# Expert layers: the output bias as a product of TensorE in place of sums of VectorE

## The chip, the cores and the metric

The kernel runs on one core of one Trainium2 chip. The metric is the device time of one execution in microseconds, the median of several runs.

## The reference

A small network of four blocks works on x of shape 16 x 96 x 16 x 16 (4096 tokens of 96 channels). Each block is a convolution or an attention part and then a feed-forward part, each added to its input. In the first three blocks the feed-forward part is a layer of four experts, which this change concerns:

```python
scores = jnp.einsum('bsd,de->bse', x, gate_w) + gate_b
probs = jax.nn.softmax(scores, axis=-1)
topk_vals, topk_idx = jax.lax.top_k(probs, TOP_K)
mask = jnp.sum(jax.nn.one_hot(topk_idx, NUM_EXPERTS, dtype=probs.dtype), axis=-2)
masked = probs * mask
masked = masked / (jnp.sum(masked, axis=-1, keepdims=True) + 1e-09)
h = jax.nn.gelu(jnp.einsum('bsd,edh->ebsh', x, w1) + b1[:, None, None, :], approximate=False)
y = jnp.einsum('ebsh,ehd->ebsd', h, w2) + b2[:, None, None, :]
out = jnp.einsum('bse,ebsd->bsd', masked, y)
```

The layer's x is the layer-normed token, DIM is 96, HID is 384, there are 4 experts and the best 2 count; the kernel computes all four and lets the gate be zero. The output bias `b2` is a row of 96 numbers for each expert, and every token receives it times its gate.

## The kernel before

The tokens X stay in SBUF as 32 tiles of 128 tokens x 96 channels. The function `moe` does one expert layer in 8 steps of 4 tiles (512 tokens). Each engine has its own program; they meet at semaphores. The first step and the last are written out, the six between them are a loop of two steps an iteration.

TensorE in step g, for experts e = 1, 2, 3: the up products of expert e (`ups`: 3 blocks of 128 hidden units, each as three reduced-precision products of 512 columns, L933 to L935), then the down products of expert e-1 (`downs`: 12 fp32 products of 96 columns, L943, into one of two PSUM banks `dn`). After the down products of expert 1 comes `turn` (L915), the transposes of the next step's normed tokens `xn`, and after the up products of expert 3 come the next step's gate products (L922). The up products of the next step's expert 0 and the down products of expert 3 end the step. The next stage's own first work stands in the last step (`follow`).

ScalarE makes the gelu (L878) between up and down products, and copies the turned tokens to `xt` and `xh`.

VectorE in step g: the 16 bias sums (`bias_sums`, L819: X = b2 * gate + X, a tile and expert each), the statistics of the next step's tokens (`stats_of`, L72 to L81), expert 0's sum (`expert_sum`, L827: X = down product * gate + X, four tiles), the normed tokens (`apply_of`, L88 to L91, which waits for a power on GpSimd, L773), expert 1's sum, the low part of the turned tokens (L806), the gates of the next step (L412 to L444, with an exponential on GpSimd, L777), and the sums of experts 2 and 3. The semaphore `added` counts the expert sums; TensorE's down products of expert e wait for the sum of expert e-2, which frees their bank.

In layer 0 the first step's statistics, tokens and gates are made inside the layer, before its steps. In layers 1 and 2 they are made in the stage before. So TensorE begins layer 1 and 2 at once with the up products of expert 0.

Of the kernel before, what the change touches and what calls it, by code (L numbers as in the profile page):

```python
# [12 lines left out]
F32 = mybir.dt.float32  # L13
# [5 lines left out]
P = 128  # L19
# [22 lines left out]
def wait(eng, sem, count):  # L42

    if isinstance(count, int) and count <= 0:
        return
    eng.wait_ge(sem, count)
# [662 lines left out]
def moe(nc, T, A, layer, follow=None):  # L709

    w1, w2, gw, b2 = T["moe"][layer]
    X, ident, F = T["X"], T["ident"], T["front"]
    w1h, w1l, xn, xt, xh, xl, gate = F.w1h, F.w1l, F.xn, F.xt, F.xh, F.xl, F.gate
# [2 lines left out]
    with ExitStack() as ctx:  # L718
        s = Scope(nc, ctx, f"moe{layer}")
        hid = s.sb("hid", [P, NE * KC, GW])  # L720
        up = [s.psum(f"up{i}", [P, 512]) for i in range(UPS)]
        tp = s.psum("tp", [P, 512])
        gp = s.psum("gp", [P, 512])
        dn = [s.psum(f"dn{i}", [P, 512]) for i in range(2)]
        scores = gp[:, 0:GT * NE]
        names = ("consts", "var_done", "rstd_done", "logit_done", "exp_done", "dve_step", "xn_done", "turned",
                 "xt_done", "xl_done", "gates_in", "gates_read", "up_done", "hid_done", "down_done", "added")
        (consts, var_done, rstd_done, logit_done, exp_done, dve_step, xn_done, turned, xt_done, xl_done, gates_in,
         gates_read, up_done, hid_done, down_done, added) = (s.sem(n) for n in names)
        if layer == 0:  # L730
            F.begin(s, T, 0, tp, scores)
        if follow:
# [54 lines left out]
        @block.vector  # L787
        def _(dve):

            STATS, APPLY, GATES = 4, 2, 15  # L790
            EACH = STATS + APPLY + GATES + 2 * NE

            def stats_of(g, chain):
                layernorm_stats(dve, chain, [X[:, GT * g + j, :] for j in range(GT)], F.stats, F.mean, F.var, 1e-5)
                dve.sem_inc(var_done, 1)  # L795

            def apply_of(g, chain):
                wait(dve, rstd_done, g)
                wait(dve, turned, g - 1)
                layernorm_apply(dve, chain, [X[:, GT * g + j, :] for j in range(GT)],  # L800
                                [xn[:, j, :] for j in range(GT)], F.stats, F.mean, F.rstd).then_inc(xn_done, 1)

            def low_of(g, p):

                wait(dve, xt_done, g)
                dve.tensor_tensor(xl[0:C, p, :], xt[0:C, p, :], xh[0:C, p, :].bitcast(F32), ALU.subtract  # L806
                                  ).then_inc(xl_done, 1)

            def gates_of(g, p, chain):
                wait(dve, gates_in, g)  # L810
                gate_logits(dve, chain, F, scores.rearrange("p (t e) -> p t e", e=NE), logit_done, gates_read)
                choose_experts(dve, chain, F, p, exp_done, g)

            def bias_sums(g, p, chain):

                for e in range(NE):
                    for j in range(GT):
                        x = X[:, GT * g + j, :]
                        last = dve.scalar_tensor_tensor(out=x, in0=b2[:, e, :], scalar=gate[:, p, j, e:e + 1], in1=x,  # L819
                                                        op0=ALU.mult, op1=ALU.add)  # L820
                    chain.sync(last)

            def expert_sum(g, p, e, chain):
                wait(dve, down_done, NE * g + e + 1)
                for j in range(GT):
                    x = X[:, GT * g + j, :]
                    last = dve.scalar_tensor_tensor(out=x, in0=dn[e % 2][:, j * C:(j + 1) * C],  # L827
                                                    scalar=gate[:, p, j, e:e + 1], in1=x, op0=ALU.mult, op1=ALU.add)
                chain.sync(last)
                dve.sem_inc(added, 1)  # L830

            def step(g, p, last):
                chain = Chain(dve, dve_step, base + g * EACH)
                begun = follow if last else None
                ahead = Chain(dve, follow.step) if begun else None
                if begun:
                    begun.dve_sums(dve, ahead)
                bias_sums(g, p, chain)
                if not last:
                    stats_of(g + 1, chain)  # L840
                if begun:
                    begun.dve_tokens(dve, ahead)
                expert_sum(g, p, 0, chain)
                if not last:
                    apply_of(g + 1, chain)
                expert_sum(g, p, 1, chain)
                if not last:
                    low_of(g + 1, 1 - p)
                    gates_of(g + 1, 1 - p, chain)
                if begun:  # L850
                    begun.dve_weights(dve, ahead)
                expert_sum(g, p, 2, chain)
                expert_sum(g, p, 3, chain)
                assert chain.n == (2 * NE if last else EACH), chain.n

            chain = Chain(dve, dve_step)
            if layer == 0:
                F.dve_stats(dve, chain)
                F.dve_apply(dve, chain)
                for e in range(NE):  # L860
                    F.dve_weights(dve, e)
                    if e == 0:
                        F.dve_low(dve)
                F.dve_logits(dve, chain)
                F.dve_gates(dve, chain)
            dve.wait_ge(T["moe_in"][layer], 64)
            base = chain.n
            steps(dve, step)

# [40 lines left out]
        def _(pe):  # L910
# [15 lines left out]
            def ups(g, p, e):  # L926
                if e == 0:
                    wait(pe, xl_done, g)
                for k in range(KC):
                    n = e * KC + k  # L930
                    wait(pe, hid_done, NE * KC * g + n - UPS + 1)
                    bank = up[n % UPS][:, :]
                    pe.matmul(bank, w1h[:, n, :], xh[:, p, :], start=True, stop=False)  # L933
                    pe.matmul(bank, w1l[:, n, :], xh[:, p, :], start=False, stop=False)  # L934
                    pe.matmul(bank, w1h[:, n, :], xl[:, p, :], start=False, stop=True).then_inc(up_done, 1)  # L935

            def downs(g, e):
                wait(pe, hid_done, NE * KC * g + (e + 1) * KC)
                wait(pe, added, NE * g + e - 1)
                for j in range(GT):  # L940
                    for k in range(KC):
                        n = e * KC + k
                        last = pe.matmul(dn[e % 2][:, j * C:(j + 1) * C], hid[:, n, j * P:(j + 1) * P], w2[:, n, :],  # L943
                                         start=(k == 0), stop=(k == KC - 1))
                last.then_inc(down_done, 1)

            def step(g, p, last):
# [20 lines left out]
            if layer == 0:  # L968
# [2 lines left out]
                pe.wait_ge(F.w_low, 1)  # L971
                pe.wait_ge(F.xl_done, 1)
            ups(0, 0, 0)
            steps(pe, step)
            if follow:
                stay_awake(pe, up[0], ident, 11)
# [1718 lines left out]
```

## Time and profile before

| | |
|---|---|
| time, median of 3 runs | 1303.06 us (1302.83 to 1305.04) |
| profiled execution | 1306.18 us, its span 1304.0 us |
| mean granted clock of TensorE | 0.952 |
| TensorE matmul busy | 1180.7 us, 91% |
| VectorE busy | 808.3 us, 62% |
| ScalarE busy | 482.9 us, 37% |
| GpSimd busy | 252.6 us, 19% |
| bias sums L819, VectorE | 384 instructions, 102.6 us |

The times come from one profiled execution. Matmul records overlap one another, so two that follow directly start closer than their duration. PEld is TensorE's weight load. "Idle before" is the time in which the engine stood still ahead of an instruction, and the arrow names what ended it. An fp32 product shows as two records.

### The profile page before, as it was taken

What the parts mean: (1) busy time and instruction counts of PE and PEld (TensorE: products, weight loads), DVE (VectorE), ACT (ScalarE), POOL (GpSimd) and SP (SyncE); (2) the same over time, 40 slices, a digit from 0 to 9 for tenths busy, and PEclk for the clock granted to TensorE, in tenths of its full rate; (3) what the DMA queues carried; (4) which work ended last, traced back from release to release, by engine and by line L of the source; (5) the groups of instructions that cost most, each with busy time, mean ns of one, the idle gap of its engine ahead of it and who ended that gap; (6) DMA issues with size and microseconds to landing.
All of it is one profiled execution on the core that took longest, in us unless ns stands there. A gap on an engine that the chain in (4) does not pass through costs nothing. (4 is left out here: it accounts for less than half of the span.)

```text
span 1304.0 us, 24105 instructions
## 1 busy us (share of the span) xinstructions
PE 1180.7 (91%) x8520; PEld 1029.8 (79%) x8520; DVE 808.3 (62%) x2930; ACT 482.9 (37%) x944; POOL 252.6 (19%) x234
## 2 busy tenths in 40 slices
PE   2979999957999999999999999999999997999776
PEld 1978888946999999888897767768988886888555
DVE  6036676736566664676666576654767667676656
ACT  3514333413455544333331323233333332232552
POOL 3002212122010100312121443332121212211200
PEclk9998999976999999899998999999999999999786
DMA  3201000010000000000000000000000000000000
GB/s 133 84 5 65 18 25 23 1 49 1 2 2 1 2 1 2 1 1 0 0 1 1 2 1 2 2 1 2 2 0 0 0 1 1 1 2 1 4 10 37
DMA packets 11562, 15.69 MB, mean 12 GB/s; under 512 B 7385, under 2 KB 9007, under 8 KB 11346
## 3 DMA queue, kind: packets, MB, share of 16 engines
q1 hardware_dynamic: 10754, 12.86, 3.0%
q10 hardware_dynamic: 720, 1.66, 0.3%
q8 instruction: 55, 0.90, 0.3%
q14 instruction: 33, 0.27, 0.1%
HBM read 11.37 MB, written 3.15 MB: 11 GB/s over the span
## 5 line engine op out<-in xcount | busy, mean ns | idle before, releaser
L943 PEld LDWEIGHTS moe_dn<-all_w,moe_hid 128*128 128x128 f32 x2304 | 269.9, 192 | 5.4
L943 PE MATMUL moe_dn<-all_w,moe_hid 128*128 128x96 f32 x2304 | 271.7, 275 | 0.0
L878 ACT ACTIVATE moe_hid<-moe_up 128x512 f32<-128x512 f32 x288 | 169.9, 599 | 231.6 <-PE moe_up L935 219.2
L933 PE MATMUL moe_up<-front_xh,front_w1h 97*128 97x512 f32 x288 | 122.4, 425 | 0.7 <-PEq L1474 0.4
L935 PE MATMUL moe_up<-front_xl,front_w1h 97*128 97x512 f32 x288 | 114.0, 396 | 0.0
L827 DVE SCALAR_TENSOR_TENSOR all_X<-moe_dn,front_gate,all_X 128x96 f32 (+1 forms) x384 | 95.2, 310 | 29.3 <-PE moe_dn L943 24.6
L934 PE MATMUL moe_up<-front_xh,front_w1l 97*128 97x512 f32 x288 | 113.4, 394 | 0.0
L819 DVE SCALAR_TENSOR_TENSOR all_X<-all_b,front_gate,all_X 128x96 f32 (+1 forms) x384 | 102.6, 329 | 13.9 <-DVE all_X L827 7.6
L1371 PE MATMUL l1c_o<-l1c_vs,l1c_pt 128*128 128x64 f32 x768 | 94.4, 277 | 0.5 <-DVE l1c_ro L1149 0.5
L1371 PEld LDWEIGHTS l1c_o<-l1c_vs,l1c_pt 128*128 128x128 f32 x768 | 91.8, 195 | 2.9 <-issue 0.9
L1115 DVE TENSOR_REDUCE l1c_nmax<-l1c_sc 128x2 f32<-128x512 f32 x96 | 61.8, 685 | 40.8 <-PE l1c_sc L1338 40.1
L777 POOL TENSOR_TENSOR front_prob<-front_euler,front_logit 128x16 f32<-128x16 f32 x21 | 60.9, 2902 | 122.3 <-DVEq L414 122.3
L1613 DVE SCALAR_TENSOR_TENSOR l2c_val<-third_xp,all_l_taps,l2c_val 96x544 f32<-96x544 f32 x64 | 64.5, 1008 | 13.8 <-ACT l2c_val L1689 11.2
L2056 DVE SCALAR_TENSOR_TENSOR l3c_ykv<-fourth_xp,all_l_taps,l3c_ykv 96x256 f32<-96x256 f32 x128 | 65.3, 510 | 4.0
L1781 PE MATMUL l2c_qp<-third_xp,third_diag 96*96 96x512 f32 x144 | 66.6, 598 | 0.0
L2182 PE MATMUL l3c_qp<-fourth_xp,fourth_wqt 96*128 96x256 f32 x288 | 66.1, 383 | 0.0
L1259 ACT ACTIVATE l1c_pt<-l1c_st 128x512 f32<-128x512 f32 x96 | 52.2, 595 | 36.9 <-PE l1c_st L1355 35.8
L935 PEld LDWEIGHTS moe_up<-front_xl,front_w1h 97*128 97x128 f32 x288 | 54.7, 190 | 12.6
L773 POOL TENSOR_TENSOR front_rstd<-front_var,front_mhalf 128x4 f32<-128x4 f32 x21 | 21.2, 1009 | 223.0 <-DVEq L795 223.0
L933 PEld LDWEIGHTS moe_up<-front_xh,front_w1h 97*128 97x128 f32 x288 | 55.4, 192 | 9.3 <-issue 1.1
L934 PEld LDWEIGHTS moe_up<-front_xh,front_w1l 97*128 97x128 f32 x288 | 55.3, 192 | 8.5
L2182 PEld LDWEIGHTS l3c_qp<-fourth_xp,fourth_wqt 96*128 96x128 f32 x288 | 54.2, 193 | 7.3
(399 smaller groups left out, 2059.0 us busy)
## 6 DMA issues: line engine op xcount, KB each, us to landing
all_w<-w SPq DMA_DIRECT2D x3, 582.0 KB
all_w<-w SPq DMA_DIRECT2D x3, 576.0 KB
all_X<-x_rows SPq DMA_DIRECT2D x2, 768.0 KB, 7.0
conv_scratch<-all_X SPq DMA_DIRECT2D x2, 768.0 KB, 3.2
all_X<-conv_scratch SPq DMA_DIRECT2D x2, 768.0 KB, 4.8
out_tokens<-l3f_y SPq DMA_DIRECT2D x5, 288.0 KB, 2.1
l0c_band<-band ACTq DMA_DIRECT2D x1, 1248.0 KB, 9.4
all_b<-b SPq DMA_DIRECT2D x3, 192.0 KB
```

The source lines that it names most:

```text
L819: last = dve.scalar_tensor_tensor(out=x, in0=b2[:, e, :], scalar=gate[:, p, j, e:e + 1], in1=x, op0=ALU.mult, op1=ALU.add)
L827: last = dve.scalar_tensor_tensor(out=x, in0=dn[e % 2][:, j * C:(j + 1) * C], scalar=gate[:, p, j, e:e + 1], in1=x, op0=ALU.mult, op1=ALU.add)
L878: act.activation(hid[:, n, :], up[n % UPS][:, :], ACT.Gelu).then_inc(hid_done, 1)
L933: pe.matmul(bank, w1h[:, n, :], xh[:, p, :], start=True, stop=False)
L934: pe.matmul(bank, w1l[:, n, :], xh[:, p, :], start=False, stop=False)
L935: pe.matmul(bank, w1h[:, n, :], xl[:, p, :], start=False, stop=True).then_inc(up_done, 1)
L943: last = pe.matmul(dn[e % 2][:, j * C:(j + 1) * C], hid[:, n, j * P:(j + 1) * P], w2[:, n, :], start=(k == 0), stop=(k == KC - 1))
L1371: last = pe.matmul(o_ps[:, at:at + VWIDE], pt[:, 2 * (n % 2) + i, m * PIX + t * P:m * PIX + (t + 1) * P], vs[:, b % RV, m, h * VW:h * VW + ...
L1613: ins = dve.scalar_tensor_tensor(out=v, in0=image, scalar=taps[:, 3, t:t + 1], in1=v, op0=ALU.mult, op1=ALU.add)
L1781: ins = pe.matmul(o, diag[:, w, t, :], images(p)[:, :, dy:dy + SIDE:stride, dx:dx + SIDE:stride], start=(t == 0), stop=(t == TAPS - 1))
L2056: ins = dve.scalar_tensor_tensor(out=y3, in0=image, scalar=taps[:, 1, t:t + 1], in1=y3, op0=ALU.mult, op1=ALU.add)
L2182: ins = pe.matmul(o, wqt[:, t, :], xp[:, b % 2, dy:dy + SIDE, dx:dx + SIDE], start=(t == 0), stop=(t == TAPS - 1))
```

## The change

The bias sums go. A step's VectorE program begins with the statistics, followed by the normed tokens (`apply_of`), and only then by the sums of experts 0 and 1. In their place each group of down products begins with one more product: a matrix of ones, 64 rows by 128, times the bias of the expert repeated four times, 64 rows by 384 columns, in reduced-precision fp32 (F32R). Row 0 holds the bias rounded to that type, row 32 what rounding lost, and the other rows are zero. The 12 down products add to it. VectorE makes these rows and the ones once a layer (`bias_rows`), after the gates of the first step, and TensorE waits for them (`bias_in`) after the up products of the first step's expert 0.

```diff
@@ -718,15 +719,19 @@
     with ExitStack() as ctx:
         s = Scope(nc, ctx, f"moe{layer}")
         hid = s.sb("hid", [P, NE * KC, GW])
+        LOW, ROWS = 32, 64
+        b2h = s.sb("b2h", [ROWS, NE, C], F32R)
+        b2rows = s.sb("b2rows", [ROWS, NE, C], F32R)
+        b2ones = s.sb("b2ones", [ROWS, P], F32R)
         up = [s.psum(f"up{i}", [P, 512]) for i in range(UPS)]
         tp = s.psum("tp", [P, 512])
         gp = s.psum("gp", [P, 512])
         dn = [s.psum(f"dn{i}", [P, 512]) for i in range(2)]
         scores = gp[:, 0:GT * NE]
         names = ("consts", "var_done", "rstd_done", "logit_done", "exp_done", "dve_step", "xn_done", "turned",
-                 "xt_done", "xl_done", "gates_in", "gates_read", "up_done", "hid_done", "down_done", "added")
+                 "xt_done", "xl_done", "gates_in", "gates_read", "up_done", "hid_done", "down_done", "added", "bias_in")
         (consts, var_done, rstd_done, logit_done, exp_done, dve_step, xn_done, turned, xt_done, xl_done, gates_in,
-         gates_read, up_done, hid_done, down_done, added) = (s.sem(n) for n in names)
+         gates_read, up_done, hid_done, down_done, added, bias_in) = (s.sem(n) for n in names)
         if layer == 0:
             F.begin(s, T, 0, tp, scores)
         if follow:
@@ -788,7 +793,7 @@
         def _(dve):
 
             STATS, APPLY, GATES = 4, 2, 15
-            EACH = STATS + APPLY + GATES + 2 * NE
+            EACH = STATS + APPLY + GATES + NE
 
             def stats_of(g, chain):
                 layernorm_stats(dve, chain, [X[:, GT * g + j, :] for j in range(GT)], F.stats, F.mean, F.var, 1e-5)
@@ -811,14 +816,14 @@
                 gate_logits(dve, chain, F, scores.rearrange("p (t e) -> p t e", e=NE), logit_done, gates_read)
                 choose_experts(dve, chain, F, p, exp_done, g)
 
-            def bias_sums(g, p, chain):
-
-                for e in range(NE):
-                    for j in range(GT):
-                        x = X[:, GT * g + j, :]
-                        last = dve.scalar_tensor_tensor(out=x, in0=b2[:, e, :], scalar=gate[:, p, j, e:e + 1], in1=x,
-                                                        op0=ALU.mult, op1=ALU.add)
-                    chain.sync(last)
+            def bias_rows(chain):
+                high, low = slice(0, 1), slice(LOW, LOW + 1)
+                chain.sync(dve.tensor_copy(b2h[:, :, :], b2[0:ROWS, :, :]))
+                chain.sync(dve.tensor_scalar(b2rows[:, :, :], b2[0:ROWS, :, :], 0.0, None, ALU.mult))
+                dve.tensor_scalar(b2ones[:, :], ident[0:ROWS, :], 0.0, 1.0, ALU.mult, ALU.add)
+                dve.tensor_copy(b2rows[high, :, :], b2h[high, :, :].bitcast(F32))
+                dve.tensor_tensor(b2rows[low, :, :], b2[low, :, :], b2h[low, :, :].bitcast(F32), ALU.subtract
+                                  ).then_inc(bias_in, 1)
 
             def expert_sum(g, p, e, chain):
                 wait(dve, down_done, NE * g + e + 1)
@@ -835,14 +840,12 @@
                 ahead = Chain(dve, follow.step) if begun else None
                 if begun:
                     begun.dve_sums(dve, ahead)
-                bias_sums(g, p, chain)
                 if not last:
                     stats_of(g + 1, chain)
+                    apply_of(g + 1, chain)
                 if begun:
                     begun.dve_tokens(dve, ahead)
                 expert_sum(g, p, 0, chain)
-                if not last:
-                    apply_of(g + 1, chain)
                 expert_sum(g, p, 1, chain)
                 if not last:
                     low_of(g + 1, 1 - p)
@@ -851,7 +854,7 @@
                     begun.dve_weights(dve, ahead)
                 expert_sum(g, p, 2, chain)
                 expert_sum(g, p, 3, chain)
-                assert chain.n == (2 * NE if last else EACH), chain.n
+                assert chain.n == (NE if last else EACH), chain.n
 
             chain = Chain(dve, dve_step)
             if layer == 0:
@@ -864,6 +867,7 @@
                 F.dve_logits(dve, chain)
                 F.dve_gates(dve, chain)
             dve.wait_ge(T["moe_in"][layer], 64)
+            bias_rows(chain)
             base = chain.n
             steps(dve, step)
 
@@ -937,11 +941,14 @@
             def downs(g, e):
                 wait(pe, hid_done, NE * KC * g + (e + 1) * KC)
                 wait(pe, added, NE * g + e - 1)
+                out = dn[e % 2][:, 0:GT * C]
+                pe.matmul(out.rearrange("p (j c) -> p j c", c=C), b2ones[:, :],
+                          b2rows[:, e, :].unsqueeze(1).broadcast_to([ROWS, GT, C]), start=True, stop=False)
                 for j in range(GT):
                     for k in range(KC):
                         n = e * KC + k
-                        last = pe.matmul(dn[e % 2][:, j * C:(j + 1) * C], hid[:, n, j * P:(j + 1) * P], w2[:, n, :],
-                                         start=(k == 0), stop=(k == KC - 1))
+                        last = pe.matmul(out[:, j * C:(j + 1) * C], hid[:, n, j * P:(j + 1) * P], w2[:, n, :],
+                                         start=False, stop=(j == GT - 1 and k == KC - 1))
                 last.then_inc(down_done, 1)
 
             def step(g, p, last):
@@ -971,6 +978,7 @@
                 pe.wait_ge(F.w_low, 1)
                 pe.wait_ge(F.xl_done, 1)
             ups(0, 0, 0)
+            pe.wait_ge(bias_in, 1)
             steps(pe, step)
             if follow:
                 stay_awake(pe, up[0], ident, 11)
```

TensorE in the first step of layer 0, where the second expert's up products begin. `moe_up` are the PSUM banks of the up products. Before:

```order
L935 MATMUL moe_up<-front_xl,front_w1h 128x512
L933 MATMUL moe_up<-front_xh,front_w1h 128x512 [waits moe0_front_w_low]
L934 MATMUL moe_up<-front_xh,front_w1l 128x512
L935 MATMUL moe_up<-front_xl,front_w1h 128x512
L933 MATMUL moe_up<-front_xh,front_w1h 128x512 [waits moe0_hid_done]
```

In the change:

```order
L939 MATMUL moe_up<-front_xl,front_w1h 128x512
L937 MATMUL moe_up<-front_xh,front_w1h 128x512 [waits moe0_front_w_low,moe0_bias_in]
L938 MATMUL moe_up<-front_xh,front_w1l 128x512
L939 MATMUL moe_up<-front_xl,front_w1h 128x512
L937 MATMUL moe_up<-front_xh,front_w1h 128x512 [waits moe0_hid_done]
```

The first up product of the second expert now waits for the bias rows as well.

TensorE later in the same step, from the last up product of expert 2 over the down group of expert 1 to the turn of the next step's tokens. Before:

```order
L935 MATMUL moe_up<-front_xl,front_w1h 128x512
L943 MATMUL moe_dn<-all_w_0,moe_hid 128x96 [waits moe0_hid_done]
L943 MATMUL moe_dn<-all_w_0,moe_hid 128x96 x11
L915 MATMUL moe_tp<-all_ident,front_xn 96x128 [waits moe0_xn_done]
L915 MATMUL moe_tp<-all_ident,front_xn 96x128 x3
```

In the change:

```order
L939 MATMUL moe_up<-front_xl,front_w1h 128x512
L945 MATMUL moe_dn<-moe_b2rows,moe_b2ones 128x384 [waits moe0_hid_done]
L950 MATMUL moe_dn<-all_w_0,moe_hid 128x96 x12
L919 MATMUL moe_tp<-all_ident,front_xn 96x128 [waits moe0_xn_done]
L919 MATMUL moe_tp<-all_ident,front_xn 96x128 x3
```

One product of 384 columns stands ahead of the 12 down products and takes over their wait.

VectorE in the first step of layer 0, from the end of its gates (L444) to the next gates, the change against before:

```order
 L444 TENSOR_TENSOR front_gate<-front_gate,front_smax 128x16
-L819 SCALAR_TENSOR_TENSOR all_X<-all_b_0,front_gate,all_X 128x96 x16
+L821 CAST moe_b2h<-all_b_0 64x384
+L822 TENSOR_SCALAR moe_b2rows<-all_b_0 64x384
+L823 TENSOR_SCALAR moe_b2ones<-all_ident 64x128
+L824 CAST moe_b2rows<-moe_b2h 1x384
+L825 TENSOR_TENSOR moe_b2rows<-all_b_0,moe_b2h 1x384
 L72 BN_STATS front_stats<-all_X 128x6 x4
 L76 TENSOR_TENSOR front_mean<-front_stats 128x4
```

Five operations of 64 or 1 rows, once a layer, stand where the first step's 16 bias sums stood; in the other steps nothing stands there. A little later on the same engine:

```order
 L81 TENSOR_TENSOR front_var<-front_var,front_mean 128x4
-L827 SCALAR_TENSOR_TENSOR all_X<-moe_dn,front_gate,all_X 128x96 x4
 L88 TENSOR_TENSOR front_mean<-front_stats 128x4
 L89 TENSOR_SCALAR front_mean<-front_mean 128x4
 L91 TENSOR_SCALAR front_xn<-all_X,front_mean,front_rstd 128x96 x4
-L827 SCALAR_TENSOR_TENSOR all_X<-moe_dn,front_gate,all_X 128x96 x4
-L806 TENSOR_TENSOR front_xl<-front_xt,front_xh 96x512
+L832 SCALAR_TENSOR_TENSOR all_X<-moe_dn,front_gate,all_X 128x96 x8
+L811 TENSOR_TENSOR front_xl<-front_xt,front_xh 96x512
```

The sum of expert 0 has moved behind the normed tokens.

## Rows read from the trace of the kernel before

**Rows 1.** The page: busy time, and the clock granted in 40 slices.
```profile
PE 1180.7 (91%) x8520; PEld 1029.8 (79%) x8520; DVE 808.3 (62%) x2930; ACT 482.9 (37%) x944; POOL 252.6 (19%) x234
...
PEclk9998999976999999899998999999999999999786
```

**Rows 2.** The page, costliest groups: the down products.
```profile
L943 PE MATMUL moe_dn<-all_w,moe_hid 128*128 128x96 f32 x2304 | 271.7, 275 | 0.0
```

**Rows 3.** Waits: total us, times, longest us.
```profile
PEld moe_tp L915 <- DVE front_xn L91: 17.5, 20, 1.3
```

**Rows 4.** Timeline, TensorE, 132.6 to 143: start, us, instruction, [idle before].
```profile
132.68 2.81 PE L943 MATMUL moe_dn<-all_w,moe_hid 128*128 128x96 f32 x24
136.23 0.64 PE L915 MATMUL moe_tp<-all_ident,front_xn 128*96 128x128 f32 x4 [0.73 <-DVE front_xn L91]
136.63 0.48 PE L933 MATMUL moe_up<-front_xh,front_w1h 97*128 97x512 f32 x1
136.95 0.40 PE L934 MATMUL moe_up<-front_xh,front_w1l 97*128 97x512 f32 x1
...
138.55 0.39 PE L935 MATMUL moe_up<-front_xl,front_w1h 97*128 97x512 f32 x1
138.78 0.95 PE L922 MATMUL moe_gp<-all_gw,front_xt 97*128 97x4 f32 x8
139.59 2.90 PE L943 MATMUL moe_dn<-all_w,moe_hid 128*128 128x96 f32 x24
```

**Rows 5.** Timeline, VectorE, 122.9 to 137.
```profile
125.00 2.13 DVE L827 SCALAR_TENSOR_TENSOR all_X<-moe_dn,front_gate,all_X 128x96 f32<-128x96 f32 x8
127.58 4.13 DVE L819 SCALAR_TENSOR_TENSOR all_X<-all_b,front_gate,all_X 128x96 f32 x16 [0.46 <-DVE all_X L827]
131.87 0.74 DVE L72 BATCH_NORM_STATS2 front_stats<-all_X 128x6 f32 x4 [0.16 <-DVE all_X L819]
...
134.72 0.17 DVE L88 TENSOR_TENSOR front_mean<-front_stats 128x4 f32<-128x4 f32 x1 [0.22 <-POOL front_rstd L773]
...
135.13 1.05 DVE L91 TENSOR_SCALAR front_xn<-all_X,front_mean,front_rstd 128x96 f32 x4
```

**Rows 6.** Timeline, TensorE, 503.95 to 505: products of 64 rows.
```profile
504.09 0.28 PE L1355 MATMUL l1c_st<-l1c_nms,l1c_selr 64*128 64x256 f32 x2
504.21 0.28 PE L1351 MATMUL l1c_st<-l1c_qk 64*128 64x256 f32 x2
```

**Rows 7.** Timelines, TensorE and VectorE, 102 to 107: layer 0 begins.
```profile
103.92 0.63 PE L933 MATMUL moe_up<-front_xh,front_w1h 97*128 97x512 f32 x1
...
106.58 0.55 DVE L819 SCALAR_TENSOR_TENSOR all_X<-all_b,front_gate,all_X 128x96 f32<-128x96 f32 x2
```

**Rows 8.** Windows: PEclk is the clock granted in each.
```profile
99.90:103.40 3.50, 3.50 (x9) 2.82 (x10) 0.73 (x7) 1.84 (x3) 2.75 (x1) 0.50 0.17 64
103.40:106.80 3.40, 3.40 (x9) 2.63 (x8) 2.77 (x18) 1.36 (x4) 0.15 (x1) 0.50 0.07 28
106.80:110.20 3.40, 3.40 (x28) 3.25 (x28) 3.29 (x15) 1.12 (x2) 0.00 (x0) 1.00 0.07 27
526.60:530.10 3.50, 3.20 (x14) 2.84 (x14) 0.94 (x4) 0.62 (x1) 0.63 (x2) 0.50 0.00 0
```

**Rows 9.** Groups by line, VectorE: total us, mean ns.
```profile
L502 DVE TENSOR_TENSOR front_w1l<-all_w,front_w1h 97x384 fp32r<-97x384 f32 x12 | 6.4, 548 | 0.2 <-DVE front_var L81 0.2
...
L1179 DVE CAST l1c_selr<-all_l_sel 128x768 fp32r<-128x768 f32 x1 | 0.5, 549 | 0.0
```

**Rows 10.** Timelines, VectorE and TensorE: layers 1 and 2 begin.
```profile
529.52 4.62 DVE L819 SCALAR_TENSOR_TENSOR all_X<-all_b,front_gate,all_X 128x96 f32<-128x96 f32 x7 [2.53 <-PEq L990]
...
531.92 0.39 PE L933 MATMUL moe_up<-front_xh,front_w1h 97*128 97x512 f32 x1
...
893.05 3.09 DVE L819 SCALAR_TENSOR_TENSOR all_X<-all_b,front_gate,all_X 128x96 f32<-128x96 f32 x12 [1.27 <-DVEq L1474]
...
895.27 0.39 PE L933 MATMUL moe_up<-front_xh,front_w1h 97*128 97x512 f32 x1
```

## The prediction

> **What bounds the kernel now.** I read the page first: TensorE is busy 91% of the span, and its granted clock is near full except in a few short stretches [rows 1]. In the three expert layers the down products are 2304 records of 275 ns (96 groups, one for each expert and step, of 12 fp32 matmuls in two records each) [rows 2]. Next the waits: in these layers the matrix engine waits in one place that counts, the turning of the next step's tokens (L915), for VectorE's layernorm result (L91). The weight loads of that line stood still 17.5 us in 20 waits, of 21 such turns in the kernel [rows 3]. The loads, not the matmuls, are the measure: a matmul's record overlaps its neighbour's, a load begins as soon as the stream can go on. Then the timeline of one step. Down products begin at 132.68; their 24 records end after 2.81 us, the last being 0.275 long, so they follow each other at (2.81 - 0.275) / 23 = 0.11 us and the turn could begin at about 135.3; it begins at 136.23, when VectorE's last L91 ends (135.13 + 1.05 = 136.18) [rows 4, 5]. Last, VectorE in the same step: the previous step's expert sums end at 127.13, then come 4.13 us of bias sums from 127.58, then statistics from 131.87, expert 0's sum beside GpSimd's power, and L91 [rows 5]. So TensorE sets the pace of the layers, and the bias sums push its one input late by about 0.9 us a step.
>
> **What is taken off.** The 16 bias sums of a step go (384 instructions in all). They cost 127.58 to 131.87, 4.3 us of VectorE, and expert 0's sum moves behind L91. Then the statistics start at 127.58. From their start to the mean operation that GpSimd's power releases it is 2.85 us (131.87 to 134.72, and expert 0's sum lay inside without lengthening it, since the wait for GpSimd ended last), to L91 another 0.41, and L91 takes 1.05. The tokens are ready at about 131.9, and TensorE asks for them at 135.3 or later: 3.4 us of margin [rows 5]. All 20 waits should go: **minus 17.5 us** [rows 3]. Both ends: 14.0 us if a fifth of it returns as waits after a loop branch, 17.5 us at most. Nothing else needs the bias sums early. Expert 0's sum is wanted only before the third down group refills its bank (139.59); it now waits for L91 to end at 131.9 and for its own down group, and is done long before [rows 4].
>
> **What is added on TensorE.** One product per expert, 8 steps and 4 experts in 3 layers: 96 products, 64 rows deep, 384 columns, reduced-precision fp32. No such row exists. The nearest: 512 columns of this type start 0.23 us apart (138.55 to 138.78) [rows 4]; 256 columns with 64 rows start 0.12 us apart [rows 6]. Halfway lies 0.175 us. The products stand between an up product and the down group, where nothing is idle. 96 x 0.175 = **plus 16.8 us**. In 21 of the groups the product parts the gate products (L922) from the down products, and the stream goes from fp32 to the other type and back once more; after such a change the next start came at 0.32 us after 136.63 instead of 0.23, less what the last fp32 product saved. I put 0.03 us on each: **plus 0.6 us**. Bounds of one product: 0.12 (the 256-column row, 11.5 us in all) and 0.175 + 0.11 = 0.286 us (27.5 us), if its weight load could not be hidden. A stream bound by its loads runs at 0.10 to 0.11 us per load: the eight records of the 4-column gate products take 138.78 to 139.59 [rows 4]. I take 0.175, since a 97-row load is hidden under each up product today: otherwise they could not follow at 0.23, which is about 512 columns at 2.4 GHz.
>
> The Trainium skill (TensorE: Matmul & The Clock Gate, Back-to-back issue gap) gives columns / 2.4 GHz plus 2.5 ns for warm products, 162.5 ns here; by it the estimate for the 96 would be 15.6 us instead of 16.8. Its sum for 512 columns would be 216 ns, where this trace shows 230, so I stay with the rows.
>
> **What is added on VectorE, and whom it holds.** Five operations make the rows, after the gates of the first step and before the statistics; TensorE waits for them before the second expert's up products. Cost by rows: a cast to this type takes 0.55 us for 768 columns, and for 384 I put 0.36, since small operations of this engine (L88) take 0.17 and the rest goes by columns; a subtraction with 384 columns is 0.55; the multiply by zero I put at 0.45, the ones at 0.33, the one-row copy at 0.36, and two waits on itself at 0.1 each [rows 5, 9]. Together 2.3 us.
> In layer 0 VectorE has finished the gates at 106.58, so the rows are there at 108.9. TensorE has ended the first expert's up products at 103.92 and today goes straight on [rows 7]. **Plus 5.0 us** of standing still. Behind that wait on TensorE stands everything of the layer; VectorE's statistics of step 1 are later too (they began 4.2 us after 106.58, now 2.3), which hurts nobody.
> That stretch ran at half clock: 0.50 from 103.4 to 106.8, full from 106.8 on, after TensorE had multiplied without a gap from 99.9; in the next layer half clock also lasted to 530.1 with TensorE busy [rows 8]. After a pause of 5 us the clock may have to be earned again. Worst, another 6.9 us at half clock, as from 99.9 to 106.8, instead of the 2.9 us of work done at half clock today: (6.9 - 2.9) / 2 = 2.0 us lost. Best, the clock rises at 106.8 all the same and the 2.9 us are done in half the time: 1.45 us won. I take **plus 1.4 us**, nearer to the worst, since the pause lies just where the clock rose.
> In layers 1 and 2 the gates are done in the stage before. VectorE starts at 529.52 and has the rows at 531.85, TensorE wants them at 531.92; in layer 2 893.05 + 2.3 = 895.35 against 895.27 [rows 10]. **Plus 0.1 us**, and at most 1 us if the five operations take half a microsecond more.
>
> **The sum.** -17.5 + 16.8 + 0.6 + 5.0 + 1.4 + 0.1 = +6.4 us. The profiled execution took 1306.18 us with a span of 1304.0; it would become 1312.6. It lies 3.1 us above the median of the runs (1303.06), and the terms are the same for those, so I forecast 1303.1 + 6.4 = **1309.4 us**. A measurement of this kernel can tell about 0.2%, 2.6 us, from no change.
>
> **The rivals.**
> *The weight load is not hidden* (slower still). A product of 64 rows could keep its own or the next 128-row load from running under it: 0.286 us each, 10.7 us more, 1320.1 us. For it: the type and the row count change at both sides of the product. Against: the 97-row and 64-row rows show hidden loads [rows 4, 6]. Chance 0.10. The Trainium skill (same page, The mechanism) says that a load overlaps a running product only when it goes to another row group, which would give this case; the up products here, whose row groups are the same, disagree.
> *The product is cheap and the clock rises anyway* (no difference). At 0.145 us, 13.9 us in all, and with the clock's best case: -17.5 + 13.9 + 0.6 + 5.0 - 1.45 + 0.1 = +0.7, 1303.7 us. Chance 0.17.
> *The product hides beside its neighbour* (faster). Products of 64 rows run in pairs on the two halves of the array: two pairs of 256 columns in 0.24 us, 0.06 each [rows 6]. If the bias product likewise runs beside the last up product or the first load-bound down product (whose 0.11 us is a load, not its columns), it costs 0.06: 5.8 us instead of 16.8, and the sum is -4.6 us, 1298.4 us. It decides below 0.08 us a product. Against it: its neighbours use 97 and 128 rows, hence both halves. Chance 0.10.
> *The waits stay.* If L91 still came late, for a reason that the timeline hides, the change would only add: up to +23.9, 1327 us. Chance 0.05; the margin of 3.4 us speaks against it.
>
> **How the numbers follow.** The forecast has 0.58; its own range is 1305.7 (product at 0.15, no clock loss) to 1313. With the case of no difference and that of the unhidden load the range is 1301 to 1320.5; outside lie the paired product and the staying waits, 0.15. Slower by over 0.2%: 0.58 + 0.10 + 0.05 = 0.73; within: 0.17; faster: 0.10.
>
> **What the changed profile would show.** No wait of L915 for L91 in the list of waits, and turns that follow the down group directly. 96 products of 64x384 whose follower starts about 0.175 us later. VectorE about 100 us less busy. In layer 0 a pause of TensorE from 103.9 to about 108.9, ended by the last of the five operations, and full clock not before some 110 to 116 us; no such pause in the other two layers. The step between two turns about 21.0 us instead of 21.2. The forecast is wrong if the follower starts within 0.11 us or after 0.25, or if the five operations take far from 2.3 us.

## The result and the profile after

The changed kernel takes 1353.85 us, median of 4 runs (1353.38 to 1357.43), against 1304.05 us of the kernel before (4 runs); the ratio is 1.038, 95% interval 1.033 to 1.042. It is slower, as forecast, but by 47.5 us in the spans (1351.5 against 1304.0) where 6.4 were forecast, and outside the range.

The page, whose lines answer to [rows 1]:

```profile
span 1351.5 us, 23854 instructions
...
PE 1233.2 (91%) x8616; PEld 1045.4 (77%) x8616; DVE 719.3 (53%) x2561; ACT 482.4 (36%) x944; POOL 252.9 (19%) x234
...
PEclk9987999987899999899999999999999999899787
```

TensorE's share is the same as before, and its mean clock nearly so (0.950 against 0.952); the extra time does not show as idleness in it. The waits (total us, times, longest us), with TensorE's at the bias rows, and the weight loads' (PEld) at the bias products (L945) and at the down products behind them (L950):

```profile
PE moe_up L937 <- DVE moe_b2rows L825: 8.8, 2, 4.5
...
PEld moe_dn L945 <- issue: 22.6, 64, 0.4
...
PEld moe_dn L950 <- issue: 18.1, 96, 0.3
```

No line of L919 (the turns, L915 before) is left, where [rows 3] had 17.5 us: that part of the forecast came true. The two load lines are new, and "issue" means that nothing the profile knows of held them. The timeline of TensorE in a step, to be laid beside [rows 4]:

```profile
122.77 0.60 PE L919 MATMUL moe_tp<-all_ident,front_xn 128*96 128x128 f32 x4
...
141.79 0.39 PE L939 MATMUL moe_up<-front_xl,front_w1h 97*128 97x512 f32 x1
142.11 0.44 PE L945 MATMUL moe_dn<-moe_b2rows,moe_b2ones 64*128 64x384 f32 x1
142.48 2.92 PE L950 MATMUL moe_dn<-all_w,moe_hid 128*128 128x96 f32 x24
145.24 0.60 PE L919 MATMUL moe_tp<-all_ident,front_xn 128*96 128x128 f32 x4
```

The product of 384 columns begins 0.32 us after the up product before it (142.11 less 141.79; an up product's follower came after 0.23), and the first down product 0.37 us after that (142.48). From turn to turn it is 22.47 us (122.77 to 145.24). The weight loads at the same place:

```profile
141.57 0.19 PEld L939 LDWEIGHTS moe_up<-front_xl,front_w1h 97*128 97x128 f32 x1
142.11 0.18 PEld L945 LDWEIGHTS moe_dn<-moe_b2rows,moe_b2ones 64*128 64x128 f32 x1 [0.35 <-issue]
142.48 0.63 PEld L950 LDWEIGHTS moe_dn<-all_w,moe_hid 128*128 128x128 f32 x5 [0.19 <-issue]
```

The load of L939 begins at 141.57, together with the product ahead of its own. The load of the bias product does not: it begins at 142.11, when the product itself does, and that of the down product at 142.48 likewise. Two loads a group are no longer under a product.

The beginnings of layer 0 and layer 1 on TensorE, for [rows 7, 10], and the clock (windows, PEclk third from the end), for [rows 8]:

```profile
103.18 0.63 PE L939 MATMUL moe_up<-front_xl,front_w1h 97*128 97x512 f32 x1
108.12 0.80 PE L937 MATMUL moe_up<-front_xh,front_w1h 97*128 97x512 f32 x1 [4.32 <-DVE moe_b2rows L825]
...
553.35 0.58 PE L937 MATMUL moe_up<-front_xh,front_w1h 97*128 97x512 f32 x1 [4.51 <-DVE moe_b2rows L825]
```

```profile
103.40:108.10 4.70, 0.40 (x1) 0.00 (x0) 4.14 (x23) 0.60 (x1) 0.00 (x0) 0.50 0.07 28
108.10:117.00 8.90, 8.88 (x30) 7.26 (x31) 2.76 (x15) 1.79 (x3) 1.01 (x1) 0.52 0.14 47
...
553.90:557.30 3.40, 3.40 (x10) 2.25 (x8) 2.05 (x13) 1.19 (x2) 1.01 (x1) 0.54 0.00 0
```

In layer 0 the pause is 4.3 us and ends at 108.12, and the half clock lasted 8.6 us more, to 116.7 (the window to 117.0 has 0.3 us at full clock in it, hence 0.52). In layer 1, where I expected none, TensorE stood 4.5 us, and 3.4 us at half clock came after it. On VectorE the five operations of layer 1, with GpSimd's work of the same time below them:

```profile
546.33 1.40 DVE L821 CAST moe_b2h<-all_b 64x384 fp32r<-64x384 f32 x1 [2.52 <-PEq L998]
547.76 1.68 DVE L822 TENSOR_SCALAR moe_b2rows<-all_b 64x384 fp32r<-64x384 f32 x1
549.48 1.54 DVE L823 TENSOR_SCALAR moe_b2ones<-all_ident 64x128 fp32r<-64x128 f32 x1
550.94 1.79 DVE L824 CAST moe_b2rows<-moe_b2h 1x384 fp32r<-1x384 f32 x1
552.75 0.55 DVE L825 TENSOR_TENSOR moe_b2rows<-all_b,moe_b2h 1x384 fp32r<-1x384 f32 x1
...
546.34 1.18 POOL L581 MEMSET third_xp<- 96x1296 f32 x1
547.60 4.92 POOL L576 TENSOR_TENSOR third_diag<-all_ident,all_l_taps 96x864 f32<-96x864 f32 x3
```

They took 7.0 us here (1.8 in layer 0, 2.3 in layer 2). Four of them last 1.4 to 1.8 us. The first ran beside a memset of GpSimd, the other three beside its three multiplications, 4.92 / 3 = 1.64 us each, and each of the four ended 0.1 to 0.2 us after the GpSimd instruction beside it.

### The profile page after: what moved, and what is told of

The parts are those of the page before. It is cut to its first block and busy times, and to the rows that moved or that the text cites. A ratio compares the mean times of both kernels' runs of the same rounds, so it can differ in the third digit from the quotient of the medians.

```text
span 1351.5 us, 23854 instructions
## 1 busy us (share of the span) xinstructions
PE 1233.2 (91%) x8616; PEld 1045.4 (77%) x8616; DVE 719.3 (53%) x2561; ACT 482.4 (36%) x944; POOL 252.9 (19%) x234
## 5 line engine op out<-in xcount | busy, mean ns | idle before, releaser
L950 PE MATMUL moe_dn<-all_w,moe_hid 128*128 128x96 f32 x2304 | 282.0, 279 | 0.0
L950 PEld LDWEIGHTS moe_dn<-all_w,moe_hid 128*128 128x128 f32 x2304 | 266.3, 193 | 18.1 <-issue 18.1
L939 PE MATMUL moe_up<-front_xl,front_w1h 97*128 97x512 f32 x288 | 115.0, 399 | 0.0
L939 PEld LDWEIGHTS moe_up<-front_xl,front_w1h 97*128 97x128 f32 x288 | 55.3, 192 | 12.9
L386 PE MATMUL l0c_cp<-l0c_xt,l0c_full 128*128 128x176 f32 (+6 forms) x312 | 56.1, 337 | 0.0
L386 PEld LDWEIGHTS l0c_cp<-l0c_xt,l0c_full 128*128 128x128 f32 x312 | 53.4, 190 | 1.3
```

What stands on the lines that cost most here:

```text
L386: last = pe.matmul(out[:, :, lo:hi], full[:, g * KL + r, :, :].rearrange("p c x -> p (c x)"), xt[:, g, :, lo + d:hi + d], start=(n == 0), ...
L950: last = pe.matmul(out[:, j * C:(j + 1) * C], hid[:, n, j * P:(j + 1) * P], w2[:, n, :], start=False, stop=(j == GT - 1 and k == KC - 1))
```

## The experiments

Two theories at the start. A: a product that needs only half of the array's rows, between products that need all of them, has no load hidden on either side. B: the gap comes from the product's moving operand (96 columns read four times) or from its writing a bank that the next products add to. The kernel before, run beside them, had medians of 1306.19 us (15 runs, first four kernels), 1307.11 (13 runs, next four) and 1307.18 (18 runs, last two), single runs from 1300.3 to 1314.5.

**1. No product.**

```diff
-                pe.matmul(out.rearrange("p (j c) -> p j c", c=C), b2ones[:, :],
-                          b2rows[:, e, :].unsqueeze(1).broadcast_to([ROWS, GT, C]), start=True, stop=False)
...
-                                         start=False, stop=(j == GT - 1 and k == KC - 1))
+                                         start=(k == 0), stop=(k == KC - 1))
```

> The changed kernel without its 96 bias products; the bias rows are still made and waited for, and the output bias is left out of the result. Both theories agree here: the products cost 0.54 us each (start to start 0.32 us before the product and 0.37 us behind it in the changed kernel's trace), so 51.8 us go, 1353.9 becomes about 1302, and a step between two turns of tokens becomes 20.3 us. If the time stays well above 1302, the 48 us lie elsewhere, in the waits at the layers' beginnings.

Measured: 1296.69 us (6 runs), ratio to before 0.991 (0.988 to 0.994). Turns of TensorE:

```profile
119.94 0.60 PE L919 MATMUL moe_tp<-all_ident,front_xn 128*96 128x128 f32 x4
...
140.22 0.60 PE L919 MATMUL moe_tp<-all_ident,front_xn 128*96 128x128 f32 x4
```

The step is 20.28 us, so the four products of a step cost 22.47 - 20.28 = 2.19 us, 0.55 each, and 96 of them 52.6 us: more than the whole slowdown. The medians differ by more, 57.2 us, and I had written about 1302 us for this run; the table further below shows that the rest does not lie in the expert layers.

**2. 128 rows.**

```diff
-        LOW, ROWS = 32, 64
+        LOW, ROWS = 32, 128
```

> The bias product 128 rows deep instead of 64, the added rows zero. Theory A (a product of 64 rows between products of 97 and 128 rows can neither have its weights loaded under its neighbour nor let the next load run under it): the product falls from 0.54 to about 0.175 us, 35 us less, about 1319 us. Theory B (the cost comes from the shape of its moving operand, one row of 96 read four times, or from writing 384 columns of a bank that the next product adds to): no change, 1353.9 us, and 0.37 us from the product to its follower.

Measured: 1315.35 us (10 runs), ratio 1.006 (1.004 to 1.008).

```profile
154.45 0.39 PE L939 MATMUL moe_up<-front_xl,front_w1h 97*128 97x512 f32 x1
154.68 0.34 PE L945 MATMUL moe_dn<-moe_b2rows,moe_b2ones 128*128 128x384 f32 x1
154.85 2.37 PE L950 MATMUL moe_dn<-all_w,moe_hid 128*128 128x96 f32 x20
```

With twice the rows the 96 products are 38.5 us cheaper by the medians, and 34.6 us by the steps (21.03 us each instead of 22.47): a product begins 0.23 us after the up product and its follower 0.17 us after it. Against the kernel without products it costs (1315.35 - 1296.69) / 96 = 0.19 us.

**3. The operand written out.**

```diff
+        b2wide = s.sb("b2wide", [ROWS, NE, GT, C], F32R)
...
-                pe.matmul(out.rearrange("p (j c) -> p j c", c=C), b2ones[:, :],
-                          b2rows[:, e, :].unsqueeze(1).broadcast_to([ROWS, GT, C]), start=True, stop=False)
+                pe.matmul(out, b2ones[:, :], b2wide[:, e, :, :].rearrange("p j c -> p (j c)"), start=True, stop=False)
```

> The bias product at 64 rows, but with its moving operand written out as 384 columns in place of 96 read four times; four more copies make it at the beginning of each layer, 0.35 us each by the trace of the change, so up to 1.5 us more waiting in a layer. Theory A: 1353.9 plus 2 to 5, about 1357 us, and 0.37 us from the product to its follower. Theory B in its first form: about 1322 us, and 0.17 us to the follower.

Measured: 1357.76 us (one run).

```profile
154.23 0.39 PE L942 MATMUL moe_up<-front_xl,front_w1h 97*128 97x512 f32 x1
154.54 0.44 PE L948 MATMUL moe_dn<-moe_b2wide,moe_b2ones 64*128 64x384 f32 x1
154.92 2.92 PE L952 MATMUL moe_dn<-all_w,moe_hid 128*128 128x96 f32 x24
```

The gaps stay. The first form of theory B falls here, and the second with experiment 2, in which the 128-row product writes the same 384 columns of the same bank.

**4. The order alone, on the kernel before.**

```diff
-                bias_sums(g, p, chain)
                 if not last:
                     stats_of(g + 1, chain)
+                    apply_of(g + 1, chain)
+                bias_sums(g, p, chain)
...
                 expert_sum(g, p, 0, chain)
-                if not last:
-                    apply_of(g + 1, chain)
```

> The kernel before with its bias sums, only moved behind the next step's statistics and normed tokens. If the 17.5 us of waits of the turns come from the place of the bias sums alone, they go: 1304 becomes about 1286.5 us, with no wait of a turn for the normed tokens. The rival: VectorE is then late with the gates and the expert sums, since the 4.2 us now stand before the sums of experts 0 and 1; the turns stop waiting but other places begin to, and the time is 1295 or more.

Measured: 1283.74 us (4 runs), ratio 0.982 (0.978 to 0.985). Two turns of TensorE, then VectorE between them:

```profile
113.14 0.60 PE L914 MATMUL moe_tp<-all_ident,front_xn 128*96 128x128 f32 x4
...
133.42 0.60 PE L914 MATMUL moe_tp<-all_ident,front_xn 128*96 128x128 f32 x4
```

```profile
125.58 0.74 DVE L72 BATCH_NORM_STATS2 front_stats<-all_X 128x6 f32 x4 [0.36 <-DVE all_X L827]
...
128.65 1.05 DVE L91 TENSOR_SCALAR front_xn<-all_X,front_mean,front_rstd 128x96 f32 x4
129.61 4.13 DVE L819 SCALAR_TENSOR_TENSOR all_X<-all_b,front_gate,all_X 128x96 f32 x16
133.78 0.99 DVE L827 SCALAR_TENSOR_TENSOR all_X<-moe_dn,front_gate,all_X 128x96 f32 x4
```

The bias sums cost the same 4.13 us and stand behind L91, whose result is there at 129.7 while the turn comes at 133.42. A step is 20.28 us, as with no bias at all (experiment 1). The rival did not come: TensorE waits nowhere in these steps. This is the version that beats both kernels.

**5. 65 rows.**

```diff
-        LOW, ROWS = 32, 64
+        LOW, ROWS = 32, 65
```

> The bias product with 65 rows instead of 64 (the added row is zero). Theory A1 (what counts is whether the product needs more than the half of the array's rows, as its neighbours with 97 and 128 rows do): 0.18 us to its follower and about 1316 us, as with 128 rows. Theory A2 (any product with fewer rows than its follower's load waits): 0.37 us to the follower and about 1354 us.

Measured: 1315.44 us (one run).

```profile
151.42 0.39 PE L939 MATMUL moe_up<-front_xl,front_w1h 97*128 97x512 f32 x1
151.65 0.34 PE L945 MATMUL moe_dn<-moe_b2rows,moe_b2ones 65*128 65x384 f32 x1
151.83 2.81 PE L950 MATMUL moe_dn<-all_w,moe_hid 128*128 128x96 f32 x24
```

One row more and 38 us less: 65 rows are as good as 128 (a step takes 21.04 us), although the loads on both sides differ in their row counts (97, 65, 128). Of the row counts tried (64, 65, 128), the one that does not go beyond 64 pays; fewer rows were not tried.

**6. The product in full fp32.**

```diff
-        b2rows = s.sb("b2rows", [ROWS, NE, C], F32R)
-        b2ones = s.sb("b2ones", [ROWS, P], F32R)
+        b2rows = s.sb("b2rows", [ROWS, NE, C])
+        b2ones = s.sb("b2ones", [ROWS, P])
```

> The changed kernel, its bias product of 64 rows, with ones and rows kept as full fp32 (two records a product). If the rows alone make the gap, it stays: the first record again begins more than 0.3 us after the up product before it, the last record's follower again waits longer than the columns ask, and the fp32 passes come on top: 1365 us or more. If the gap came from the reduced-precision type beside fp32 loads of the same rows, it goes, and a product costs its two passes of 384 columns at two cycles each, about 0.64 us in place of 0.54: about 1363 us, with the next load under the last pass.

Measured: 1395.47 us (one run), 41.6 us above the changed kernel. Its product has two records of 64 rows, 0.43 and 0.41 us to their followers, and it begins late behind the up product as before. The type is not the cause. My price for the fp32 product was too low.

**7. Two products a group.**

```diff
                           b2rows[:, e, :].unsqueeze(1).broadcast_to([ROWS, GT, C]), start=True, stop=False)
+                pe.matmul(out.rearrange("p (j c) -> p j c", c=C), b2ones[:, :],
+                          b2zero[:, :].unsqueeze(1).broadcast_to([ROWS, GT, C]), start=False, stop=False)
```

> A second product of 64 rows (zeros) directly behind the first, in each of the 96 groups. Theory A (the cost lies in the two changes of the row count, not in the product): the second costs 0.175 us, 16.8 us in all, about 1371 us, and the two follow each other at 0.17 to 0.19 us. Theory C (each product of 64 rows and 384 columns has the gap of its own): 0.37 us each, 35.5 us, about 1389 us.

Measured: 1377.05 us (one run), 23.2 us above the changed kernel.

```profile
149.27 0.40 PE L941 MATMUL moe_up<-front_xl,front_w1h 97*128 97x512 f32 x1
149.59 0.44 PE L947 MATMUL moe_dn<-moe_b2rows,moe_b2ones 64*128 64x384 f32 x1
149.88 0.34 PE L949 MATMUL moe_dn<-moe_b2zero,moe_b2ones 64*128 64x384 f32 x1
150.14 2.02 PE L954 MATMUL moe_dn<-all_w,moe_hid 128*128 128x96 f32 x16
```

From the first product to the down group it is 0.55 us (149.59 to 150.14) where one product had 0.37: the second costs 0.18, 17.3 us in all. The rest of the 23.2 goes with the clock: TensorE was at half clock for 9.6 us more of this run (mean 0.947 against 0.950), 4.8 us of full-clock time; in layer 0 half clock lasted to 130.3 instead of 116.7. The two do not follow each other at 0.17 as I had written (0.29 and 0.26 us), but their sum is that of theory A, not of C.

**8. Bias rows made earlier and awaited later (128 rows).**

```diff
                         F.dve_low(dve)
+                bias_rows(chain)
...
-            bias_rows(chain)
+            if layer > 0:
+                bias_rows(chain)
...
             def downs(g, e):
+                if isinstance(g, int) and g == 0 and e == 0:
+                    pe.wait_ge(bias_in, 1)
...
             ups(0, 0, 0)
-            pe.wait_ge(bias_in, 1)
```

> The 128-row version with its bias rows made earlier in layer 0 (ahead of the gates) and waited for only at the first down group, in each layer. Against the 128-row version (1315.4 us): in layer 0 the pause of 4.4 us goes, and the half clock ends at about 106 instead of 113 to 117 us, worth 2 to 3 us more; in layer 1 the wait shrinks from 4.6 to some 2.5 us; in layer 2 nothing. About 1306 us. If the pauses at the beginnings cost nothing beyond their length, 1309; if they are given back elsewhere, 1315.

Measured: 1312.3 us (10 runs, 1306.3 to 1314.3), ratio 1.003 (1.000 to 1.005). Windows of layer 0's beginning:

```profile
95.00:105.50 10.50, 9.10 (x27) 7.36 (x28) 5.45 (x22) 5.99 (x10) 2.90 (x1) 0.50 0.25 79
105.50:120.00 14.50, 14.50 (x107) 13.59 (x107) 7.67 (x43) 5.64 (x10) 2.96 (x2) 1.00 0.12 39
```

The timeline of TensorE in layer 1:

```profile
535.37 0.51 PE L949 MATMUL moe_dn<-moe_b2rows,moe_b2ones 128*128 128x384 f32 x1 [2.57 <-DVE moe_b2rows L825]
```

The pause of layer 0 is gone and the clock is full from 105.5 instead of 113 to 117 us, but layer 1 keeps a wait of 2.57 us, and the medians fell by only 3.0 us where I had written 9. In the traces the 9 us are there: the three layers together took 9.8 us less than in experiment 2 (500.7 and 490.9 us, see the table below). The spans differ by only 6.9 us (1316.4 and 1309.5), because outside the layers this execution had 11 us more at half clock (125.5 against 114.3). Why the clock was granted otherwise there, no run shows.

**9. GpSimd later (128 rows).**

```diff
             if follow:
+                pool.wait_ge(bias_in, 1)
                 follow.pool_weights(pool)
```

> The 128-row version, with GpSimd's preparation for the next stage (its memsets and the large multiplications in layers 1 and 2) begun only after the bias rows are made. In the trace of the change the five operations took 2.0 us in layer 0, 7.0 in layer 1 and 2.3 in layer 2, and in layer 1 GpSimd's three multiplications of 1.6 us ran in the same 7 us. If the two engines hold each other up, the five take about 2.0 us in layer 1 too, TensorE's wait there of 4.6 us shrinks to under 0.3, and the time falls from 1315.4 by 4.5 to 6.5 us to about 1310. If the five are slow in layer 1 for another reason (first use of their code there), they still take 7 us and the time stays 1315.

Measured: 1308.7 us (10 runs), 6.6 us less than experiment 2; ratio 1.001 (1.000 to 1.003).

```profile
532.05 0.36 DVE L822 CAST moe_b2h<-all_b 128x384 fp32r<-128x384 f32 x1 [2.52 <-PEq L999]
...
533.34 0.55 DVE L826 TENSOR_TENSOR moe_b2rows<-all_b,moe_b2h 1x384 fp32r<-1x384 f32 x1
...
533.95 0.13 POOL L580 MEMSET third_mhalf<- 128x32 f32 x1 [17.62 <-DVE moe_b2rows L826]
535.26 4.83 POOL L576 TENSOR_TENSOR third_diag<-all_ident,all_l_taps 96x864 f32<-96x864 f32 x3
```

Of the five operations the first and the last stand here; from 532.05 to 533.89 all five take 1.8 us where they took 7.0, with nothing changed but GpSimd's start. GpSimd's three multiplications take 4.83 us here and took 4.92 beside the five operations: it was VectorE that was held up, hardly GpSimd. TensorE's wait in layer 1 is gone.

**10. All repairs (128 rows).** The edits of experiments 2, 8 and 9 together.

> All repairs together: 128 rows, bias rows early in layer 0, waited for at the first down group, and GpSimd's preparation after them. No waits for the bias rows are left; against before the 17.5 us of the turns are saved and 96 products of 0.19 us added: -17.5 + 18.5, so 1304 to 1307 us, no faster than before, and some 22 us slower than the bias sums left on VectorE but moved.

Measured: 1306.0 us (10 runs), ratio 0.999 (0.997 to 1.001). The idea with these repairs is worth nothing: the products give back what the waits had cost.

## Why the prediction was wrong

The sign held, the sum did not, and the sign held in part by luck. In my sum the waits and the products cancel (-17.5 + 16.8 + 0.6 = -0.1), and the whole forecast of a slowdown hung on the 6.5 us at the layers' beginnings; in the measurement most of it comes from the products. The kernel that my sum really priced is that of experiment 2, 9.2 us slower than before by the medians. Two of the prediction's own signs of being wrong came: a follower more than 0.25 us behind the product (0.37), and a pause in a second layer.

To check the terms, the traces are cut at the first and the last up product of each of the three expert layers (us, from one profiled execution of each; 90 of the 96 products lie within):

| kernel | three layers | of this at half clock | all the rest | of this at half clock |
|---|---|---|---|---|
| before | 488.4 | 7.4 | 815.6 | 118.0 |
| the change | 533.4 | 21.0 | 818.1 | 114.7 |
| 1, no product | 485.0 | 22.1 | 808.3 | 99.1 |
| 2, 128 rows | 500.7 | 20.6 | 815.7 | 114.3 |
| 4, order only | 469.9 | 6.3 | 810.9 | 108.3 |
| 8, early rows | 490.9 | 10.2 | 818.6 | 125.5 |
| 9, GpSimd later | 491.9 | 13.1 | 814.0 | 112.4 |
| 10, all repairs | 489.3 | 12.6 | 817.6 | 119.0 |

With each us at half clock counted as half a us, the rest takes 756 to 761 us in all of them; its time at half clock differs, and this moves the spans by several us. So the terms are compared within the layers. Term by term, against the traces:

- "All 20 waits should go: minus 17.5 us": right. None is left, and by the order alone (experiment 4) the layers become 18.5 us shorter. The medians fell by 22.4 us; the rest lies outside the layers.
- **"96 x 0.175 = plus 16.8 us": this step failed.** The products cost 52.6 us (experiment 1; the layers' 48.3 us for the 90 products in them give 0.54 each, as the steps do). I priced the 64-row product by a row of 64-row products among themselves and by 97-row products among themselves, and argued that "a 97-row load is hidden under each up product today". The case here is the change from more than 64 rows to 64 and back. At each change the load waits for the product ahead (the load rows above), and experiments 2 and 5 remove exactly this: 0.19 us a product at 128 rows, near my 0.175. The rival *The weight load is not hidden* named the mechanism, but its 0.286 us, my upper bound, was built as one load's 0.11 us more. Measured: 0.09 more ahead of the product, 0.37 instead of 0.17 behind it, and the rest of 0.55 at the first down product. Two loads that nothing hides would make 0.22 us at the 0.11 us of a load-bound stream, an estimate; the product at 64 rows costs 0.36 us more than at 128. What the other 0.14 us is, no run here shows.
- The trace of the kernel before had a sign of it, one row above and two below those I quoted as [rows 6]. Timeline, TensorE:

```profile
503.86 0.39 PE L1351 MATMUL l1c_st<-l1c_qk 64*128 64x256 f32 x2
...
504.44 0.40 PE L1338 MATMUL l1c_sc<-l1c_qk 64*128 64x256 f32 x4
504.77 0.38 PE L537 MATMUL l1c_m<-all_gw,front_xt 97*128 97x4 f32 x2
```

  L1351 at 503.86 is the first pair of 64-row products behind 128-row ones (L1371), and its follower came at 504.09, 0.23 us later, not 0.12. The two pairs of L1338 should take 0.24 us; the next product, of 97 rows, came after 0.33.
- "Plus 0.6 us" for the change of the type in 21 groups: nothing is left of it in the end. In experiment 2 the product behind the gate products takes 0.26 us to its follower instead of 0.17 (123.70 to 123.96), but the down group behind it is 0.09 us shorter than in experiment 1 (2.59 against 2.68).
- "Plus 5.0 us of standing still" in layer 0: 4.3. The five operations took 1.8 us, not 2.3.
- "Plus 1.4 us" for the clock in layer 0: half clock lasted 8.6 us after the pause, 2.9 before the change, so (8.6 - 2.9) / 2 = 2.9 us. That is beyond my worst (2.0), which took the earlier stretch as the longest possible. It is no fixed price either: behind the same pause half clock lasted 4.6 us in experiment 9, 5.2 in experiment 2, 6.8 in experiment 1 and 21.6 in experiment 7. What decides it, no run here shows.
- "Plus 0.1 us" in layers 1 and 2, "at most 1": **failed too**. Layer 1 cost 4.5 us of waiting and 1.7 us for 3.4 us at half clock. I priced the five operations by their lengths on a quiet engine. GpSimd's preparation of the next stage ran beside them and held them up (experiment 9). The first row of [rows 10] said it: seven bias sums in 4.62 us, 0.66 each, where the same sums took 0.26 elsewhere. The whole of it, on VectorE and GpSimd of the kernel before:

```profile
529.52 8.31 DVE L819 SCALAR_TENSOR_TENSOR all_X<-all_b,front_gate,all_X 128x96 f32<-128x96 f32 x16 [2.53 <-PEq L990]
...
530.78 4.84 POOL L576 TENSOR_TENSOR third_diag<-all_ident,all_l_taps 96x864 f32<-96x864 f32 x3
```

  Sixteen sums took 8.3 us, not the 4.13 of [rows 5]: three of them, beside GpSimd's three multiplications, last 1.7 us each, the others 0.31 to 0.32. The Trainium skill (SBUF — State Buffer, Terms) says that VectorE and GpSimd share one pair of ports that one instruction holds to its end; the traces agree, with VectorE operations that end 0.1 to 0.2 us after GpSimd's, each of which lasts 1.6 us. In the kernel before, the three multiplications end at 530.78 + 4.84 = 535.62, 3.7 us after TensorE wants the rows (531.92); this could have been read ahead of the result, and the wait measured 4.5.

Together: -17.5 + 52.6 + 4.3 + 2.9 + 4.5 + 1.7 = 48.5 us, against 47.5 between the spans. Of the 42.1 us by which my sum of 6.4 fell short of these 48.5, the product's price makes 35.8 and layer 1 6.1; the clock in layer 0 adds 1.5, the pause there and the term for the type take 1.3 back.

Of the rivals, the paired product and the cheap one are refuted. The rule of the Trainium skill (TensorE: Matmul & The Clock Gate, The mechanism) that a load runs beside a product only in another row group is too broad for these traces, since up products of the same rows overlap; but it pointed at the right place, and I gave it 0.10.

## What to carry to other kernels

A product's price is that of its place in the stream: take it from a row where the same change of shape happens, not from rows of equal neighbours. When a wait names a late input, first try to move the work that delays it; here that gave 1.8% for a few moved lines, while moving the work to the bound engine gave nothing even with every repair that was tried. When two runs differ by a few us, compare the stage that was changed before the spans, since the clock elsewhere differs too. A new operation at a stage's beginning is priced with what the other engines do at that moment.

## What the runs showed of the hardware

- A product of 64 rows between products of 97 and 128 rows costs 0.55 us for 384 columns; one of 65 or 128 rows 0.19 us. Padding with zero rows past 64 saved 38 us (35 us by the steps). A second 64-row product behind the first costs 0.18 us.
- VectorE's casts and multiplications by a constant, of 0.22 to 0.36 us with GpSimd idle, took 1.5 to 1.8 us beside GpSimd's multiplications and 1.4 us beside its memset. The bias sums took 1.7 us beside the multiplications and their usual 0.31 to 0.32 beside the memset. GpSimd's multiplications took 4.92 us instead of 4.83.
- After the pause of 4.3 us in layer 0, taken at half clock, TensorE stayed at half clock 8.6 us more, and in other kernels with this pause (4.3 to 4.4 us) between 4.6 and 21.6 us; without it (experiment 8) the clock was full from 105.5 us. The pause of 4.5 us in layer 1, at full clock, was followed by 3.4 us at half, and that of 4.7 us in experiment 2 by 6.7 us.
